# Value matmuls of an attention step issued as one piece in the diagonal steps of a float32 causal attention kernel

## The reference, cut to what matters

```python
# x: (4, 2048, 256) float32; 16 heads of 16 dimensions
x = x + attention(layernorm(x), Wq, Wk, Wv, Wo)
x = x + ffn(layernorm(x), w1, b1, w2, b2)          # 256 -> 1024 -> 256, relu

def attention(x, Wq, Wk, Wv, Wo):
    Q, K, V = heads(x @ Wq.T), heads(x @ Wk.T), heads(x @ Wv.T)   # (4, 16, 2048, 16)
    Q, K = rope(Q), rope(K)
    scores = Q @ K.T / 4
    scores = where(key > query, -inf, scores)                     # causal
    return merge(softmax(scores) @ V) @ Wo.T
```

## Time and profile before

| what | value |
|---|---|
| median of 2 runs | 2064.44 us (2060.8 to 2068.07) |
| profiled execution, device time | 2068.45 us |
| its span from first to last instruction | 2066.7 us |
| TensorE busy, share of the span | 95% |
| VectorE busy | 89% |
| ScalarE busy | 73% |
| GpSimd busy | 30% |
| granted TensorE clock, mean | 0.971 |

### The profile page before, as it was taken

The page is one execution under the profiler, slowest core; times in us unless marked ns, Lnnn a source line. Parts: engine busy times, 40 slices in busy tenths (PEclk is TensorE's granted clock), DMA queues, the critical chain, the costliest instruction groups (busy, mean ns, idle before and its releaser), DMA issues. The chain is left out here.

```text
span 2066.7 us, 54533 instructions
## 1 busy us (share of the span) xinstructions
PE 1958.2 (95%) x20128; PEld 821.6 (40%) x20128; DVE 1835.6 (89%) x3190; ACT 1515.4 (73%) x3253; POOL 627.5 (30%) x1252
## 2 busy tenths in 40 slices
PE   6887799999999999999999999999999889999998
PEld 3444133232333333333333333333333156777776
DVE  7999999999999999999999999999997057777775
ACT  6995298887899888988889888898888623333332
POOL 8998022324221222212222122221212223333331
PEclk9998599999999999999999999999999689999999
DMA  5666533030312304123041230412301112222220
GB/s 206 229 241 216 113 74 69 18 70 18 80 38 55 70 18 80 37 56 70 18 80 36 57 69 19 80 34 58 69 8 35 55 64 86 86 85 81 84 84 26
DMA packets 133607, 153.49 MB, mean 74 GB/s; under 512 B 23936, under 2 KB 99712, under 8 KB 133120
## 3 DMA queue, kind: packets, MB, share of 16 engines
q1 hardware_dynamic: 133376, 150.46, 28.2%
HBM read 90.64 MB, written 59.77 MB: 73 GB/s over the span
## 5 line engine op out<-in xcount | busy, mean ns | idle before, releaser
L960 ACT ACTIVATE s_prob<-s_ps 128x512 f32<-128x512 f32 (+3 forms) x2560 | 1200.1, 536 | 159.8 <-PE s_ps L829 131.6
L208 DVE TENSOR_REDUCE part_max<-s_ps 128x2 f32<-128x1024 f32 (+3 forms) x1024 | 1082.7, 1117 | 13.6 <-PE s_ps L191 8.0
L829 PE MATMUL s_ps<-aq,ak 64*128 64x512 f16 (+3 forms) x2560 | 764.9, 355 | 4.4 <-ACT s_prob L960 1.7
L848 PE MATMUL s_ps<-s_prob,s_v 128*32 128x256 f32 (+3 forms) x10240 | 745.3, 363 | 0.0
L191 PE MATMUL s_ps<-mk,mq 64*128 64x512 f16 (+3 forms) x2560 | 654.0, 358 | 43.0 <-DVE part_max L208 34.9
L990 POOL TENSOR_SCALAR_AFFINE_SELECT s_prob<-s_prob 128x128 f32<-128x128 f32 x1024 | 292.1, 294 | 1105.6 <-ACT s_prob L960 1093.5
L829 PEld LDWEIGHTS s_ps<-aq,ak 64*128 64x128 f16 x2560 | 196.5, 94 | 478.2 <-ACT s_prob L960 413.2
L848 PEld LDWEIGHTS s_ps<-s_prob,s_v 128*32 128x32 f32 x10240 | 202.7, 108 | 392.1 <-issue 229.4
L215 DVE CUSTOM_DVE_ANT_0 s_ps<-s_ps,mask_sb 128x512 f32<-128x512 f32 (+3 forms) x512 | 241.4, 510 | 17.4 <-PE s_ps L191 16.9
L191 PEld LDWEIGHTS s_ps<-mk,mq 64*128 64x128 f16 x2560 | 156.5, 93 | 117.9 <-DVE part_max L208 98.5
L1263 ACT ACTIVATE s_h_f<-s_ps,s_b_s 128x512 f32<-128x512 f32 x128 | 88.0, 687 | 107.0 <-PE s_ps L1128 86.0
(11 more groups left out here) (103 smaller groups left out, 1772.9 us busy)
## 6 DMA issues: line engine op xcount, KB each, us to landing
v_scratch<-s_vst SPq DMA_DIRECT2D x32, 512.0 KB, 3.7
s_v<-v_scratch SPq DMA_DIRECT2D x16, 1024.0 KB, 12.2
att_scratch<-s_o SPq DMA_DIRECT2D x64, 256.0 KB, 2.5
aq<-qk_scratch SPq DMA_DIRECT2D x96, 128.0 KB, 4.4
ak<-qk_scratch SPq DMA_DIRECT2D x96, 128.0 KB, 7.2
s_xin<-x SPq DMA_DIRECT2D x16, 512.0 KB, 4.2
qk_scratch<-s_r_lo SPq DMA_DIRECT2D x64, 128.0 KB, 1.9
qk_scratch<-s_r_hi SPq DMA_DIRECT2D x64, 128.0 KB, 2.0
```

Of the source, the lines that this page charges most:

```text
L208: nc.vector.tensor_reduce(ops.part[:, qt // TPC, :, pair, qt % TPC, kc], ps[:, bank_of(use):bank_of(use) + 2, 0:w], AX.X, ALU.max).then_in ...
L829: nc.tensor.matmul(ps[:, s_bank(s, j), q0:CH], ak[rows, p, j // 2, kb * P:(kb + 1) * P], aq[rows, p, j // 2, c * CH + q0:(c + 1) * CH], st ...
L848: last = nc.tensor.matmul(ps[32 * j:32 * j + 32, O_BANK, cols], v[:, p, kb, j, :], prob_of(i, s)[:, j, cols], start=kb == 0 and part == 0, ...
L960: nc.scalar.activation(prob_of(i, s)[:, j, q0:CH], ps[:, s_bank(s, j), q0:CH], ACT.Exp, scale=1.0 / (SQK * DK ** 0.5)).then_inc(p_done, 1)
```

## The change

In diagonal steps, all columns of the value matmuls are issued in one piece with couple 0, and none with couple 1. The other steps keep their two halves. `pv_step` and `value_step` get a parameter for it, and the semaphore `pv_done` is raised by the last matmul of the one piece. What the value matmuls wait for, and which step they belong to (two behind), stays.

```diff
-            def pv_step(i, p, s, part):
+            def pv_step(i, p, s, part, parts=2):
...
-                cols = slice(q0 + half * part, q0 + half * (part + 1))
+                cols = slice(q0 + half * part, q0 + half * (part + 1)) if parts == 2 else slice(q0, CH)
                 for j in range(G):
 
                     last = nc.tensor.matmul(ps[32 * j:32 * j + 32, O_BANK, cols], v[:, p, kb, j, :],
                                             prob_of(i, s)[:, j, cols], start=kb == 0 and part == 0,
-                                            stop=kb == TPC * (c + 1) - 1 and part == 1)
-                if part == 1:
+                                            stop=kb == TPC * (c + 1) - 1 and part == parts - 1)
+                if part == parts - 1:
                     last.then_inc(pv_done, 1)
...
                             max_pair(nc, pe, ops, ps, t, pair, (0,))
-                            value_step(i, p, s, pair)
+                            if is_diagonal(s):
+                                if pair == 0:
+                                    value_step(i, p, s, 0, 1)
+                            else:
+                                value_step(i, p, s, pair)
                         continue
```

More of the change, by code:

```diff
@@ L849, in pv_step, with value_step @@
                                             prob_of(i, s)[:, j, cols], start=kb == 0 and part == 0,
-                                            stop=kb == TPC * (c + 1) - 1 and part == 1)
-                if part == 1:
+                                            stop=kb == TPC * (c + 1) - 1 and part == parts - 1)
+                if part == parts - 1:
                     last.then_inc(pv_done, 1)
-            def value_step(i, p, s, part):
+            def value_step(i, p, s, part, parts=2):
                 if s >= BEHIND:
-                    pv_step(i, p, s - BEHIND, part)
+                    pv_step(i, p, s - BEHIND, part, parts)
                 elif i > 0:
-                    pv_step(i - 1, 1 - p, NS + s - BEHIND, part)
+                    pv_step(i - 1, 1 - p, NS + s - BEHIND, part, parts)
             def iteration(i, p, use):
```

## The result

The changed kernel takes 2102.77 us (median of 2 runs, 2101.03 to 2104.5) against 2064.44: a ratio of 1.0188, with a 95% interval of 1.0136 to 1.0241. It is slower, inside the range of the prediction and 8 us under its 2111. So it is slower by 1.8 to 1.9%, where 2.3% was forecast. This is just within the 2% that one measurement can tell from no change, though both intervals lie clear of 1.

A forecast was written before the change was run, and what follows sets the result against it. VectorE was taken to bound the kernel. Its losses, 15 × 3.04 + (0.57 + 0.70) = 46.9 us, added to 2068.45 gave 2115.3 for the profiled execution and 2111 for the median; the range for all was 2076 to 2127.

The forecast's parts named there:

- VectorE has nothing to catch up with there: Bulk attention steps run at VectorE's pace, about 2.27 us; what it loses elsewhere is lost for the whole program.
- 2.05 us: VectorE's marked idle time in a steady iteration, 86.34 - 84.29; the pool from which any gain would have to come.
- The size of the piece: Diagonal-step value pieces: 512 columns take 1.00 us, 384 take 0.79; two half-width pieces take 1.14 and 0.92, saving 0.14.
- The ring: Diagonal steps: value piece, score tile 2, exponential, score tile 1, value piece; tile 2 to tile 1 takes 1.09 to 0.62 us.
- The chunks: VectorE's delay at each chunk's diagonal steps: 0.57, 0.70, 0.74 and 1.03 us, together 3.04 us an iteration.
- the 0.70: Steps 8 to 11 lose 1.03 us, but VectorE's 0.38 idle afterwards is mostly used up; taken between 0.65 and 1.03.
- The sum: All attention iterations: 15 × 3.04 + (0.57 + 0.70) = 46.9 us slower, 2115.3 for the profiled execution, 2111 as median.
- the shorter ring: Rival for diagonal steps: second max tile slips past, shorter pieces or later recovery; price 10 to 38 us, about 2095; chance 0.25.
- the prediction's own case: The ring delays VectorE at the chunks' diagonal steps; 2111 us, own range 2100 to 2124, chance 0.58.
- tile 1 of step 40: Score tile after the last diagonal step, expected at 1029.46 + 0.62 = 1030.08 against 1029.60 now, so VectorE remains the bound.
- The faster case: Rival at score and value block boundaries: TensorE counts, 0.23 us a step saved; 2032, perhaps 2022 us; chance 0.10.
- The longer ring: Rival for diagonal steps: long float32 value pieces save nothing; price 47 + 28 = 75 us, 2139; chance 0.07.

The follow-up runs named there:

- e2: Changed kernel with head 2's exponential in diagonal steps, from the second iteration on, taken over the first 64 columns only; 2088.63 us (1 run), steady iteration 87.62 us.
- e3: Kernel before the change with the same short exponential of head 2 in diagonal steps; 2059.52 us (1 run), steady iteration 86.29 us.
- e9: Against the kernel before: one value piece only in steps 0 and 1 of an iteration, halves elsewhere; 2055.61 us (1 run), steady iteration 86.27 us.
- e8: Changed kernel with its one piece moved behind couple 1 and head 0's exponential in diagonal steps cut to 64 columns; 2081.70 us (1 run).

## Why the prediction was right

**The bound.** "VectorE has nothing to catch up with there": right. No bulk step changed, and the loss of each chunk went through to the end of the iteration. One term is mislabelled: 2.05 us is all of VectorE's idle time in an iteration, but its marks make only 4 × 0.26 + 0.38 = 1.4; the rest is in gaps too short to be marked.

**The size of the piece.** 1.00 us for 512 columns on a line through two narrower ones, measured 1.00 (1044.87 to 1045.87); 0.79 for 384, measured 0.79 (1051.50 to 1052.29).

**The ring.** The value pieces were put at 1024.44, 1026.66 and 1028.67; less the shift of 22.86 they stand at 1024.43, 1026.65 and 1028.64. e2 with its control e3 shows that it is a ring through the exponential. The wait between the exponential's end and the tile was given 0.07 us and is 0.06.

**The chunks.** From a chunk's first diagonal reduction to the first full one after it, means of ten iterations:

| chunk | before | changed | difference | forecast |
|---|---|---|---|---|
| 0 | 7.80 | 8.30 | 0.50 | 0.57 |
| 1 | 7.49 | 8.18 | 0.69 | 0.70 |
| 2 | 7.74 | 8.47 | 0.72 | 0.74 |
| 3 | 7.76 | 8.76 | 1.00 | 1.03 |

Together 2.91 us against 3.04. The 0.38 us ahead of the reduction after chunk 1 are gone in the changed kernel, as the 0.70 had it.

**The sum.** The forecast for the attention stage was 46.9 us, the traces have 43.2 + 1.2 = 44.4. The medians differ by 38.3 only. The term that failed is one that I didn't have: everything outside the diagonal steps was taken as the same, and it wasn't. The last 20 steps ran at a granted clock of 0.72 in the profile of the kernel before and at 0.86 in that of the changed one (-6.2 us), and stage 2 began 1.9 us sooner. The clock of the last 20 steps differs between executions of one kernel (0.86 and 1.00 in the changed one), but it isn't mere chance either, since the changed kernel had the higher mean clock in nearly all executions. Nothing in the prediction or in the runs ties these two terms to the ring. Because of them the chances did worse than the mechanism: a time over 2105.7 us, 2% above the kernel before, was given 0.52 and one within 2% 0.44, and it came out within. And 2102.77 is only 0.8 us above the range of the shorter ring (2074 to 2102), so that the time alone couldn't have told it from the prediction's own case (2100 to 2124); the traces do.

**A wait that I missed.** I expected TensorE's tile 1 of step 40 at 1030.08. In the changed kernel tile 0 of step 40 starts only at 1053.14 - 22.86 = 1030.28, with "[0.57 <-ACT s_prob L964]". The bank of the first tile of an iteration was used last by tile 3 of the step before (160 tiles in three banks, counted anew in each iteration), so it waits for the exponential of the tile just before it. The rule of the third tile before, as the description of the kernel has it, doesn't hold there. It cost nothing, since VectorE wasn't ready earlier (1031.14).

**The rivals.** The faster case fell: of the 0.23 us that a step was to save on TensorE the pieces show 0.14 (1.00 in place of 2 × 0.57), the rest wasn't measured by itself; and e9, where the saving comes without a ring, turns two steps of it into 0.05 us an iteration. The rule that a change of the tiling mode drains TensorE (the Trainium skill, TensorEngine Tiling (Array Packing), Key Properties) isn't contradicted by the trace: those 0.14 us are saved, on an engine that isn't the bound. No run here separates the drain from the rest of a piece's fixed time. The shorter ring fell too: the second max matmul doesn't slip past the waiting tile (both at 1049.21). The longer ring fell by the piece's 1.00 us. A fourth score bank, which would open the ring itself, was not tried.

## What to carry to other kernels

Work that nobody waits for at once (here the value matmuls, two steps behind) can be the filler that covers another engine's round trip; putting it in one lump uncovers that round. Before merging such work, count the tiles between two lumps against the banks. Here four tiles stood against three banks, so one of them waited for a full round through ScalarE, and what stood behind it on TensorE's queue was late with it. And where the bound is an engine that the merged one feeds, as VectorE was here, look for the longest stretch in which it gets nothing, and not at the sum of work.

## What wasn't expected of the hardware

- The last 20 steps, with TensorE busy for 41 to 53 us in them, took 42.7, 48.1 or 54.3 us with a granted clock of 1.00, 0.86 or 0.72. Within the profiles of ten kernels this is the largest difference outside the change. The clock's records have only full (2.4 GHz) and half (1.2 GHz): in the kernel before it was at half for 30.7 us from 1605.6 us on, after TensorE had been busy for 57.6 of the 60 us ahead of that at full clock. In e8 it fell to half for a few us in three of the steady iterations, which took 1.2 to 1.4 us longer than the mean of the others.
- Stage 1 is the same code in all kernels, yet stage 2 starts at 240.1 to 240.2 us in three of the eleven profiles and at 238.3 to 238.4 in eight; the difference arises in the first 44 us and stays. It seems to go with the program and not with the execution, but only the changed kernel was profiled twice (238.3 both times). The cause is open.
